# Causal attention with two heads over the partitions, masks added partly by VectorE, and q and k stored as stacks

## What is computed

```python
Xn = (X - mu) * jax.lax.rsqrt(var + EPS) * ln_g + ln_b
Q, K, V = split_heads(Xn @ Wq + bq), split_heads(Xn @ Wk + bk), split_heads(Xn @ Wv + bv)
scores = jnp.einsum('bhqd,bhkd->bhqk', Q, K) / jnp.sqrt(jnp.float32(D_HEAD))
causal = jnp.tril(jnp.ones((n_ctx, n_ctx), dtype=bool))
A = jax.nn.softmax(jnp.where(causal, scores, -jnp.inf), axis=-1)
AV = jnp.einsum('bhqk,bhkd->bhqd', A, V)
return AV.swapaxes(-2, -3).reshape(...) @ Wo + bo
```

## Time and profile before

| | us |
|---|---|
| median of 3 runs | 1622.28 |
| lowest and highest | 1619.24, 1633.52 |
| the profiled execution | 1626.69 |
| its span in the trace | 1625.0 |

### The profile page before, as it was taken

One profiled execution on the slowest core, in us unless ns is written; L12 is line 12 of the kernel. 1 busy time (PEld: TensorE's weight loads), 2 busy tenths in 40 slices (PEclk: granted clock), 3 DMA queues, 4 the chain that ended last, 5 costly groups with the idle time before them and its releaser, 6 DMA issues. The chain is left out here.

```text
span 1625.0 us, 23544 instructions
## 1 busy us (share of the span) xinstructions
PE 1295.9 (80%) x6028; PEld 905.4 (56%) x6028; DVE 781.8 (48%) x2451; ACT 378.8 (23%) x746; POOL 383.9 (24%) x478
## 2 busy tenths in 40 slices
PE   4859999648799999796997647910999999999960
PEld 2435555436688887653554534510677677767640
DVE  6746666277412212253442564401555555655546
ACT  1205455333211212021332111100222222222210
POOL 0042222432100000001000204774233333333320
PEclk9959999879999999998999758965899999999985
DMA  3598786411980000055442201223999999999959
GB/s 109 219 178 115 119 124 94 101 52 63 295 266 1 0 0 0 23 195 174 128 132 71 69 1 56 103 110 113 276 309 308 296 299 298 312 294 297 299 177 323
DMA packets 189717, 260.04 MB, mean 160 GB/s; under 512 B 43887, under 2 KB 119375, under 8 KB 189655
## 3 DMA queue, kind: packets, MB, share of 16 engines
q1 hardware_dynamic: 141847, 190.33, 43.2%
q10 hardware_dynamic: 35568, 34.74, 7.3%
q0 software_dynamic: 12240, 34.23, 5.9%
HBM read 173.11 MB, written 85.78 MB: 159 GB/s over the span
## 5 line engine op out<-in xcount | busy, mean ns | idle before, releaser
L1553 PE MATMUL experts_ps_gu<-experts_wgu,experts_xt 128*128 128x352 f32 x636 | 218.4, 466 | 4.1 <-DMA experts_wgu<-L_ffn_w_gate_up 3.0
L1689 POOL DMA_INDIRECT y_parts<-experts_y,experts_at x159 | 152.6, 960 | 290.9 <-DVE experts_y L1645 287.9
L701 DVE TENSOR_REDUCE att_mx<-att_ps 128x1 f32<-128x512 f32 (+3 forms) x240 | 151.9, 654 | 135.4 <-PE att_ps L568 67.1
L564 PE MATMUL att_ps<-att_ks,att_qs 96*128 96x512 f32 (+4 forms) x384 | 157.3, 475 | 30.0 <-DMA att_ks<-k_parts 27.2
L1574 PE MATMUL experts_ps_y<-experts_wd,experts_ht 96*128 96x256 f32 x636 | 164.0, 380 | 0.0
L1596 ACT ACTIVATE experts_xt<-experts_ps_x 128x256 f32<-128x256 f32 x159 | 61.1, 384 | 417.1 <-PE experts_ps_x L1542 409.8
L661 ACT ACTIVATE att_pt<-att_ps 128x1024 f32<-128x1024 f32 (+3 forms) x160 | 121.9, 766 | 134.5 <-PE att_ps L586 134.3
L1553 PEld LDWEIGHTS experts_ps_gu<-experts_wgu,experts_xt 128*128 128x128 f32 x636 | 121.1, 192 | 49.1 <-DMA experts_wgu<-L_ffn_w_gate_up 4.3
L564 PEld LDWEIGHTS att_ps<-att_ks,att_qs 96*128 96x128 f32 (+1 forms) x384 | 78.3, 207 | 94.3 <-issue 61.4
L1542 PE MATMUL experts_ps_x<-all_ident,experts_x 128*128 128x128 f32 x318 | 64.6, 285 | 70.6 <-DMA experts_x<-x_sorted 70.6
L1383 POOL DMA_INDIRECT x_sorted<-all_rows,moe_slots x96 | 96.8, 1008 | 92.1 <-DVE moe_slots L1376 63.1
(11 more groups left out here) (202 smaller groups left out, 2051.5 us busy)
## 6 DMA issues: line engine op xcount, KB each, us to landing
experts_wgu<-L_ffn_w_gate_up SPq DMA_DIRECT2D x159, 352.0 KB, 5.6
experts_wd<-L_ffn_w_down SPq DMA_DIRECT2D x159, 176.0 KB
experts_x<-x_sorted ACTq DMA_DIRECT2D x159, 136.0 KB, 5.3
x_sorted<-mlp_w_empty SPq DMA_DIRECT2D x26, 816.0 KB, 10.6
att_qs<-q_parts SPq DMA_DIRECT2D x112, 128.0 KB, 3.3
att_ks<-k_parts SPq DMA_DIRECT2D x112, 128.0 KB, 5.3
combine_got<-y_parts ACTq DMA_DIRECT2D x24, 512.0 KB, 9.5
q_parts<-qkv_hi SPq DMA_DIRECT2D x8, 512.0 KB, 2.9
```

The source lines that it names most:

```text
L564: ins = pe.matmul(out, qs[a][z][0:rows_a, h, i * P:(i + 1) * P], ks[a][z][0:rows_a, h, 0:width(i)], start=a == 0, stop=a == last_part and ...
L701: dve.tensor_reduce(mx[:, hs[0]:hs[-1] + 1, i], ps_1[:, (u.c * ng + g) % 2, 0:len(hs) * width(i)] .rearrange("p (h w) -> p h w", h=len(hs) ...
L1553: ins = pe.matmul(ps_gu[:, u.bank, 0:2 * FE], xt[:, u.bank, k, :], wgu[u.slot][:, k, :], start=k == 0, stop=k == KD - 1)
L1689: pool.indirect_dma_start(out=parts_dram[:, :], out_offset=bass.IndirectOffsetOnAxis(ap=at[u.slot][:, 0:1], axis=0), in_=y[u.slot][:, :], ...
```

## The change

**The stacks are laid out in DRAM.** `project_qkv` gets `stacked`, the order of the parts of q (hi, hi, lo) and of k (hi, lo, hi). DRAM then holds [16 heads, 48 rows, 2048 tokens], and each chunk's q and k are stored by 12 DMAs of 256 KB (3 parts x 2 halves of the features, for q and k) instead of 4 of 512 KB; all 12 must land before `hi` and `lo` are written again. The store of v is unchanged.

**Attention of layer 0 is a function of its own**, `causal_attention`. Two heads m = 0, 1 stand on partitions 0 to 49 and 64 to 113 (48 rows of parts and 2 for the maxima). Every score matmul has 48 or 50 rows in one half of the array, and two with one head each follow one another into two PSUM banks. `ps_1` has three banks in turn, `ps_tr` is gone, and the two transposes use banks of `ps_1`. Loads are 4 DMAs of 192 KB on 48 partitions. For query blocks 0 and 1 PE lays the mask over the whole bank first (bf16 matmuls of 256 and 512 columns) and adds the scores; for blocks 2 and 3 PE makes no mask, and DVE adds `mask_wide` while it takes the maximum (`tensor_tensor_reduce`). The maxima are split by 4 small operations instead of 2 and go to q by 4 DMAs instead of 2. DVE's loop over the units is written out. Layer 1 keeps `attention`, and `make_constants` fills larger masks.

```diff
@@ project_qkv, SP @@
+                    for place, part in enumerate(stacked[j] if stacked else ()):
+                        t = (hi, lo)[part]
+                        for k in range(KD):
+                            rows = dst[k * heads // KD:(k + 1) * heads // KD, place * hd:(place + 1) * hd, :]
+                            sp.dma_start(rows[:, :, bass.ds(c * CHUNK, CHUNK)],
+                                         t[:, j, k, :].bitcast(F32)).then_inc(qk_stored, 16)
-                    for part, t in enumerate((hi, lo)):
+                    for part, t in enumerate(() if stacked else (hi, lo)):
@@ project_qkv, DVE and ACT, before hi and lo are written again @@
-                wait(dve, qk_stored, c * 64)
+                wait(dve, qk_stored, c * 16 * n_stores)
@@ causal_attention @@
+Q_PARTS, K_PARTS = (0, 0, 1), (0, 1, 0)
+WIDE = (1, 0)
+        masked_scores = s.sbuf("masked_scores", [P, 2, S])
+        ps_1 = s.psum("ps_1", [P, 3, S])
@@ SP @@
+                for dram, stack in ((q_dram, qs), (k_dram, ks)):
+                    for m in range(2):
+                        src = dram[bass.ds(g * hu, hu), :, bass.ds(b * S, S)].rearrange("(r m) d t -> m d r t", m=2)
+                        sp.dma_start(stack[z][m * half:m * half + of_parts, :, :].bitcast(F32), src[m])\
+                            .then_inc(qk_loaded[z], 16)
@@ POOL @@
+            for z in range(SLOTS):
+                pool.memset(ks[z][:, :, :].bitcast(F32), 1.0).then_inc(ones_set[z], 1)
@@ PE @@
+            def scores_q(u, i, r, place, ready):
+                ready()
+                w = width(i)
+                each = (r,) if i >= 2 else (0, 1)
+                outs = [ps_1[:, bank_of(place + m), 0:len(each) * w] for m in range(2)]
+                if i in WIDE:
+                    for m in range(2):
+                        pe.matmul(outs[m], ident_bf[:, :], masks(i), start=True, stop=False)
+                for a, r in enumerate(each):
+                    for m in range(2):
+                        at = slice(m * half, m * half + of_parts)
+                        ins = pe.matmul(outs[m][:, a * w:(a + 1) * w], qs[z][at, r, i * P:(i + 1) * P],
+                                        ks[z][at, r, 0:w], start=i not in WIDE, stop=i not in WIDE or a == len(each) - 1)
+                ins.then_inc(s1_done, 1)
+            def scores_k(u, j, r):
+                wait(pe, exp_done, u.n * nx + n - 1)
+                for m in range(2):
+                    at = slice(m * half, m * half + depth)
+                    ins = pe.matmul(ps_2[:, n % 2, m, 0:S - off(j)], ks[z][at, r, j * P:(j + 1) * P],
+                                    qs[z][at, r, off(j):S], start=True, stop=True)
+                ins.then_inc(s2_done, 1)
+                scores_q(u, 3, 0, 0, maxima(8))
+                scores_k(v, 0, 0)
+                values(t, 2)
+                scores_q(u, 3, 1, 2, maxima_and_output(9))
+                scores_k(v, 0, 1)
+                scores_q(w, 2, 0, 4, maxima(11))
+                scores_k(v, 1, 0)
+                values(t, 3)
+                scores_q(w, 2, 1, 6, maxima(13))
+                scores_k(v, 1, 1)
+                turn_maxima(u, maxima(14))
+                scores_q(w, 1, 0, 10, maxima_and_copy(16))
+                scores_k(v, 2, 0)
+                values(v, 0)
+                scores_k(v, 2, 1)
+                scores_q(w, 0, 0, 12, maxima(17))
+                scores_k(v, 3, 0)
+                turn_output(t, before_output)
+                values(v, 1)
+                scores_k(v, 3, 1)
@@ DVE @@
+                for m in range(2):
+                    bank = ps_1[:, bank_of(place + m), 0:len(each) * w]
+                    if i in WIDE:
+                        out = mx[:, m, each[0]:each[-1] + 1, i]
+                        ins = dve.tensor_reduce(out, bank.rearrange("p (h w) -> p h w", w=w), AX_X, ALU.max)
+                    else:
+                        wait(dve, max_done, done - 1 + m)
+                        for a, r in enumerate(each):
+                            ins = dve.tensor_tensor_reduce(
+                                out=masked_scores[:, m, a * w:(a + 1) * w], in0=bank[:, a * w:(a + 1) * w],
+                                in1=mask_wide[:, S - w:S], scale=1.0, scalar=NEG, op0=ALU.add, op1=ALU.max,
+                                accum_out=mx[:, m, r, i:i + 1])
+                    ins.then_inc(max_done, 1)
```

313 lines of the change are left out of this document (296 added, 17 removed).

## The result

The kernel after takes 1688.2 us (median of 4 runs, 1681.37 to 1690.83) against 1621.26 us before: a ratio of 1.039, 95% interval 1.033 to 1.045.

What follows compares the result with a forecast made beforehand. It took attention as a chain of PE and DVE rounds, neither engine full, with projection stores mostly hidden. From 1626.7: stores +30, units +8, loads -3, less 4.4 from profiled execution to median, gave 1657 us, range 1612 to 1690.

Steps and rivals of the forecast that it cites:

- the falling clock: Rival, attention: PE's clock falls for good, units of 13.5 to 15.7 us, +25 to +58 us; chance 0.17.
- the prediction's own sign: Attention: the prediction is wrong if a unit is under 11 or over 13.5 us.
- Stores: Projection: q and k stores run at half rate, 184 GB/s; attention starts at some 119.5 instead of 89.34, +30 us.
- v's tail: End of the projection: v's store adds 1.4 us before attention starts, on engines partly free.
- The rival of full-rate stores: Projection: stores stay at full rate, +4.5 us instead of +30, 1614 to 1632 us in all; chance 0.22.
- Loads: Start of attention: fewer loads on more partitions bring the first score sooner, -3 us (-5 to 0).
- First half of the unit: Attention, blocks 3 and 2: eight masks gone, rounds DVE-bound, 5.6 to 7.3 us, taken as 6.2.
- the fear of 0.87: Attention's first half: upper bound of 0.87 us for a 512-key maximum if each waits for the one before.
- the walk: Attention's second half, blocks 1 and 0: the steps followed in PE's order take 5.3 us.
- the failed step: Attention's clock: a unit of 12.4 us, between 11.2 and 13.5, with part of the clock's loss in it; +8 us.
- The rival that they don't run side by side: Rival, attention: score pairs don't overlap, the clock holds, a unit takes 12.3 to 12.8 us, inside the forecast; no separate chance.
- 0.6 us in its 11.2: Attention: 10 changes between half-height tiles and full array cost some 0.6 us of an 11.2-us unit.

Runs made afterwards that it cites:

- experiment 2: Kernel after with the same twelve stores of 256 KB a chunk written onto 128 rows, and attention loading by twelve DMAs a unit: 1660.5 us.
- experiment 3: Kernel after with 8 added matmuls of 512 columns a unit on PE, ahead of the key-side scores of blocks 0 and 1: 1714.6 us.
- experiment 8's second kernel: Kernel after with old stores and layout, values earlier in PE's order, and all masks in VectorE's maxima: 1644.9 us.
- experiments 5: Kernel after with old stores and layout, PE masking the long blocks again, over the whole bank (1681.8 us) or on the diagonal (1664.2 us).
- 7: Kernel after with old stores and layout, and all masks in VectorE's maxima, none on PE: 1645.0 us.
- experiment 8's first kernel: Kernel after with old stores and layout, and the values of blocks 0 and 1 earlier in PE's order: 1628.8 us.
- experiment 9's kernel: Kernel after with old stores and layout, values earlier in PE's order, and SP issuing the maxima ahead of the last three q and k loads: 1622.3 us.
- 4: Kernel after with old stores and layout and 8 added PE matmuls a unit ahead of the key-side scores of blocks 0 and 1: 1673.0 us.

## Why the prediction was right, and where its size was off

The direction and the two causes were right. The size was not: the sum gave 1657, and the measured 1688 lies within the range because the range took in the lower half of a rival (the falling clock, 0.17), and by 2 us. By the prediction's own sign, a unit of over 13.5 us, its account of the unit was wrong: a unit takes 13.7.

- **Stores: right.** The half rate was taken from the load of scales, and the burst shows 0.49 to 0.53. The start of attention moved by 34.0 us for the 30 of the sum. The first chunk takes 21.9 us instead of 20.8 (36.30 to 58.21), and v's tail was set too low: it is issued at 115.46 and attention starts at 123.38, 7.9 us later, where I had 1.4 after the last store. (Its terms, 117.7 and 1.4, make 119.1 and not 119.5.) The rival of full-rate stores is out; experiment 2 shows what it would have taken.
- **Loads: right.** -2.7 for -3.
- **First half of the unit: too low.** I took 6.2 us. From the first score at 221.19 to block 1's masks at 228.13 it is 6.9. DVE's rounds were priced at the low end or under it (0.69 and 0.56 us with a read of 0.08, of which one round to the next takes 0.61 to 0.68 for 512 keys and 0.48 for 384), so the fear of 0.87 was empty. What was missing: the split takes 1.08 us (last maximum's end at 224.27, next maximum at 225.35), block 2's second pair can start only when a bank of its first is read (0.31 of idle DVE), and block 1's masks wait for ScalarE's copy of the turned maxima (0.82 in the line at 228.13), a wait that the diff adds by putting the turned maxima in a bank of `ps_1`.
- **Second half: the walk was too long at full clock, and the clock wasn't full.** The walk gave 5.3 us (its terms make 5.2 at most). At full clock this half takes 4.7 (experiment 3), and here 6.7, because it begins in the stretch at 1.2 GHz: masks 1.01, scores 0.80 and values 1.93 us. VectorE's idle time before block 1's maxima, for which I named 1.3 us as the sign, is 2.15. With 6.2 and 5.3 the sum's unit was 11.5, not the 11.2 that it went on with; and with 6.9 and 4.7 the unit would be 11.6, level with before. That is an estimate from these rows: no unit of the kernel after ran at full clock throughout.
- **The clock: the failed step.** I walked 13.5 us for a unit half at 1.2 GHz and 15.7 for one wholly so; 13.7 and 16.4 were measured. The mechanism and its price were there, but I put 12.4 into the sum, the middle of what no row decided, and 0.17 on the case. Thirteen units then cost 31 us more than before, instead of 8. With 13.5 in the sum it would have come to 1674 (the prediction's 1679 to 1710 for this rival lies 3 to 5 us over its own terms, 1622.3 + 30 - 3 + 25 and + 58). The rows that I had at hand showed a fall after a thin stretch, and a thin half was just what the change made.
- **Pairs.** The rival that they don't run side by side is out: L943 with 512 keys, two matmuls, takes 0.44 us in the line at 221.19, as one did before. Nor does a change between half-height tiles and others leave a gap in the trace, for which the prediction had 0.6 us in its 11.2, a term that no run shows: in the kernel after, the weights of the values are loaded from 221.79 on, while the key side's pair ends at 221.87:

```profile
221.47 0.40 PE L962 MATMUL att_ps<-att_qs,att_ks 50*128 50x512 f32 x2
...
221.79 0.16 PEld L976 LDWEIGHTS att_ps_o<-att_pt,att_vs 128*32 128x32 f32 x8 [0.36 <-issue]
```

  The Trainium skill ("TensorEngine Tiling (Array Packing)", Key Properties) speaks of tiles working in parallel, which the trace bears out, and of a drain at a change of mode, of which these lines show no cost. The ends of matmuls are modelled, so a cost of a few hundredths of a us would not be seen.
- **Is it the clock or the path?** Both, and they work on each other. The clock by itself is shown by experiment 8's second kernel (11.4 and 13.7 us a unit, same code) and by the second half of the unit (6.7 us, and 4.7 at full clock in experiment 3). The path by itself is shown by experiments 5 (higher clock, no gain) and 7 (lower clock, a gain). Experiment 8's first kernel moves only where PE's work stands, and takes back the whole loss of the attention. What stays open is why the clock's pattern differs between units of the same program (five long units beside nine of 10.4 to 10.6 in experiment 9's kernel): no run separates this. The 3 us that the rest of the program gained were not looked into either.

## What to carry to other kernels

Taking work from PE cost time here, since its granted clock fell where it got thin and the work after it then ran at half speed. Look in which part of a loop an engine gets thin, and fill that part with work that has to be done anyway, from the part where others wait for it; work that need not be done made it slower (experiments 3 and 4). Look at a store's two shapes, not only its bytes: with 8 as the outer dimension on one side the DMA share was 0.49 instead of 1.04. Where one queue issues both far-ahead loads and data needed at once, put the urgent ones between the loads.

## What the hardware showed that I had not expected

- The granted clock fell and rose once per unit in the kernel after (13.7 us, a mean of 0.75) for eight units on end, and later stayed at 0.50 for 44 us with the same instructions, PE being busy 39.64 of 44.20 us by the profile.
- Two score matmuls of 48 rows and 512 columns, one in each half of the array, together took 0.44 us, the time of one of 96 rows.
- The four DMAs of the maxima, 4 KB each, took SP 0.69 us apiece to issue (2.74 for four), against 0.44 for a load of 64 KB (1.31 for three).
- A maximum with an added mask, one source in PSUM and one in SBUF, took 688 ns for 512 columns (mean of 48, 175 to 340 us), the same as the plain maximum's 686; the read of its result takes 83 ns more, of which a part overlaps the next.
